# Writing the state products of a chunked scan to four column tiles of TensorE

## The chip, the cores and the metric

The kernel runs on one core of one Trainium2 chip. The metric is the device time of one launch in microseconds, lower is better. One further execution was profiled; all the rows below are read from its trace.

## The reference, cut to what matters

Eight images of 512 channels and 32 by 32 pixels go through four residual stages (L0 to L3), each `x = x + stage(groupnorm(x))`. L0, L2 and L3 are 1x1 convolutions (L0 with a local correlation beside it). L1 is a state space block: a 512 to 1536 projection, a short convolution along the tokens, a selective scan, gates, and a 512 to 512 projection. The scan is what the change touches:

```python
def step(h, inp):
    dA_t, dB_t, x_t, C_t = inp
    h = dA_t[:, :, None, :] * h + dB_t[:, :, None, :] * x_t[..., None]
    y_t = jnp.einsum('bhds,bhs->bhd', h, C_t)
    return (h, y_t)
```

There are 2 heads, 8 states per channel, 256 channels per head and N = 1024 tokens, in an order of each head's own.

## The kernel before, in words

Five engines run programs written out by hand, with semaphores between them (`wait` at L238). `image` is called for image 0, then in a loop for images 1 to 6, two at a time, then for image 7. The order of an engine's work is the order of its calls.

The scan of a head is done in 8 chunks of 128 tokens. A chunk adds to the state what its own tokens contribute: an 8 x 256 matrix, the **state product** of this chunk. It is one fp32 matmul with K = 128 tokens, 8 columns of weights (the slice `pfac[:, c * P + far : ... + S]`) and 256 moving columns (the channels). `FAR_GROUP` is (0, 0), so `far` is 0 for both heads. There are 7 per head (the last chunk's is not needed), 14 per image. The trace shows each fp32 matmul as two weight loads and two matmuls, so 28 records per image, 224 in all.

The order on TensorE in `image` around them, per head h:

- `scan_sums(h)`: sums of the time steps into banks 7 and 0. The last of its matmuls writes all of bank 0 and, for h = 1, waits until DVE has done six steps of head 0's state chain (semaphore `h_st`).
- pieces of the input projection (`piece(n)` is n steps of three fp16 matmuls with 512 columns each), with the transposes `factor_rows` (L1825) among them.
- `scan_inner(h)`: state products of chunks 0 to 3; eight 128 x 128 fp32 products of the factors into two banks; state products of chunks 4 to 6. Chunk 6 writes where chunk 0 was, and waits for `h_st` 2 of its head. `dh_mm` is raised after chunks 1, 3, 5 and 6.
- for head 0: `scan_sums(1)`, four steps of the projection, `scan_y(0)`. For head 1: a transpose of a bound (L1885), six steps, a one-row matmul that spreads the bound (it waits for DVE's L1075), then `scan_y(1)`, which gives the scan's output and waits for ACT's evacuations (L729).

`dh_bank` puts the products of chunks 0 and 1 into the two halves of a bank's free dimension, 2 and 3 into another's, 4 and 5 into bank 0, and 6 into the first bank again. All of them stand on PSUM partitions 0 to 7.

On DVE `scan_states(h)` is a chain over the chunks: a copy (L1544) and six dependent scalar_tensor_tensor steps (L1547), each `hst[c] = hst[c - 1] * gam[c] + product[c]` on 8 partitions and 256 elements, each waiting for the one before; then two additions (L1553) that make the matrix that `scan_y` needs. For head 0 the masks of head 1 (L1482 to L1486) stand ahead of that chain on DVE. Behind a head's chain, `scan_y(h)` reads `hst`. The output of head h goes through ACT (L729), a store to DRAM, and row gathers on POOL (L482), which bring the tokens back in image order for TensorE's transposes at L1902. POOL also builds a diagonal matrix (L471) in each head.

All matmuls other than transposes go through the helper at L1599.

Of the kernel before, what the change touches and what calls it, by code (L numbers as in the profile page):

```python
# [16 lines left out]
S, HEADS = 8, 2  # L17
DH = C // HEADS
# [63 lines left out]
def build(nc, d):  # L82
    at, packed = constants()
    with ExitStack() as ctx:
# [89 lines left out]
        ps = [ctx.enter_context(nc.psum_tensor(f"bank{i}", [P, HALF], F32)) for i in range(8)]  # L174
# [10 lines left out]
        dh_bank = lambda h, c: ((3, 4, 0, 3), (5, 6, 0, 5))[h][c // 2]  # L185
# [52 lines left out]
        def wait(eng, name, m, n):  # L238

            if n:  # L240
                eng.wait_ge(s[name], m * per[name] + n)
# [577 lines left out]
        def _(eng):  # L819
# [8 lines left out]
            c = 1  # L828
# [410 lines left out]
            def image(m, z, last=False):  # L1239
# [76 lines left out]
                if not (first or last):  # L1316
                    bias(m + 1, 0)
                scan_states(m, 0)
                scan_factors(m, 1, z)
                y_largest(m)  # L1320
                scan_states(m, 1)
                y_scale(m)

# [206 lines left out]
            def scan_states(m, h):  # L1530

                far = FAR_GROUP[h] * S
                hp = slice(far, far + S)
                if h == 0:
                    wait(eng, "h_zero", m, 1)
                else:
                    wait(eng, "y_mm", m, 4 * h)
                for c in range(NT - 1):
                    wait(eng, "dh_mm", m, 4 * h + c // 2 + 1)
                    inc = ps[dh_bank(h, c)][0:S, (c % 2) * DH:(c % 2 + 1) * DH]  # L1540
                    if c == 1:
                        wait(eng, "fac_gam", m, h + 1)
                    if c == 0:
                        eng.tensor_copy(hst[hp, 0, :], inc).then_inc(s["h_st"], 1)  # L1544
                    else:
                        wait(eng, "h_st", m, 7 * h + c)
                        STT(hst[hp, c, :], hst[hp, c - 1, :], gam[:, h, c:c + 1], inc, ALU.mult, ALU.add).then_inc(s["h_st"], 1)  # L1547

                wait(eng, "fac_diag", m, h + 1)
                for half in range(2):  # L1550
                    wait(eng, "mm_m", m, 2 * h + half + 1)
                    c = slice(half * HALF, (half + 1) * HALF)
                    TT(mmat[:, c], ps[m_bank[h] + half][:, :], diag[:, c], ALU.add).then_inc(s["m_ev"], 1)  # L1553
# [43 lines left out]
        def _(eng):  # L1597
            def mm(out, lhsT, rhs, start, stop, **kw):
                return eng.matmul(out, lhsT, rhs, start=start, stop=stop, skip_group_check=True, **kw)  # L1599
# [114 lines left out]
            def image(m, z, last=False):  # L1714
# [114 lines left out]
                def state_products(h, chunks):  # L1829

                    far = FAR_GROUP[h] * S
                    for c in chunks:
                        if c < 4 and c % 2 == 0:
                            wait(eng, "fac_ptq", m, 4 * h + 1 + c // 2)
                        if c == 4:
                            wait(eng, "fac_8", m, 5 * h + 1)
                        if c == 6:
                            wait(eng, "h_st", m, 7 * h + 2)
                        ins = mm(ps[dh_bank(h, c)][0:S, (c % 2) * DH:(c % 2 + 1) * DH],
                                 pfac[:, c * P + far:c * P + far + S], rows4[:, h, c, 0:DH], True, True)  # L1840
                        if c % 2 == 1 or c == NT - 2:
                            ins.then_inc(s["dh_mm"], 1)

                def scan_inner(h):

                    state_products(h, range(0, 4))
                    for half in range(2):
                        wait(eng, "fac_ptq", m, 4 * h + (3 if half == 0 else 4))
                        for c in range(4 * half, 4 * half + 4):
                            ins = mm(ps[m_bank[h] + half][:, (c % 4) * P:(c % 4 + 1) * P], pT[:, c * P:(c + 1) * P],  # L1850
                                     qT[:, c * P:(c + 1) * P], True, True)
                        ins.then_inc(s["mm_m"], 1)
                    state_products(h, range(4, NT - 1))
# [52 lines left out]
                def out_part(u, k):  # L1906
                    o, c = out_unit_of(u)
                    out, oc = ps[out_bank[u]][:, :], slice(o * P, (o + 1) * P)
                    if k >= 2:
                        return mm(out, w_out[:, k - 2, oc], gate[:, k, c], False, k == KC - 1)  # L1910
                    hi, lo = y_pair[:, k, u // KC, 0, :], y_pair[:, k, u // KC, 1, :]
                    mm(out, w_hi["out"][:, k, oc], hi, k == 0, False)
                    mm(out, w_hi["out"][:, k, oc], lo, False, False)
                    return mm(out, w_lo["out"][:, k, oc], hi, False, False)
# [37 lines left out]
                for u in range(5, 8):  # L1952
# [4 lines left out]
                    for k in range(KC):  # L1957
                        ins = out_part(u, k)
# [122 lines left out]
```

## Time and profile before

| | us |
|---|---|
| median of 3 runs | 1782.38 |
| the 3 runs | 1779.83 to 1783.09 |
| the profiled execution, its time | 1799.47 |
| its span (first to last instruction) | 1797.7 |
| TensorE busy in it | 1702.6 |
| DVE busy | 1148.6 |
| ACT busy | 892.4 |
| POOL busy | 412.0 |

The granted TensorE clock is 0.986 of full speed over the span. In rows of the timeline the first number is the start in us from the span's start, the second the length in us of what is merged in the row, then engine, line, operation, output and input names, shapes as stationary rows * columns and moving partitions x columns, and the count. In brackets stands the idle time of the engine before it and what ended it. A matmul's own length in a row contains the passage through the array, so that matmuls of a dense stream overlap: the distance from start to start is what one costs.

### The profile page before, as it was taken

Reading aid. Unit: us, or ns where it says so; the run is one execution under the profiler, and the core shown is the slowest. Engines: PE = TensorE matmul, PEld = TensorE weight load, DVE = VectorE, ACT = ScalarE, POOL = GpSimd, SP = SyncE. Lnnn points to the kernel's source line nnn. Section 1 sums busy time; section 2 is a strip of 40 time slices with the busy share of each in tenths; the row PEclk is TensorE's granted clock in tenths of the full one; section 3 lists DMA queues with packets and bytes.
Section 4 is the critical chain, followed back from the end, with each engine's and each line's share of the span. In section 5 each row is a group of like instructions: output and inputs, shape, how many; then the busy total and the mean of one; then the engine's idle time right before and its main releaser. Section 6 shows DMA issues by size and latency. Waiting matters only on the chain.

```text
span 1797.7 us, 24269 instructions
## 1 busy us (share of the span) xinstructions
PE 1702.6 (95%) x8725; PEld 944.7 (53%) x8725; DVE 1148.6 (64%) x2232; ACT 892.4 (50%) x1091; POOL 412.0 (23%) x423
## 2 busy tenths in 40 slices
PE   4689899999999999999999999999999999999988
PEld 3255554555545555456545565455554565555643
DVE  6879585656754666546865568555675467652675
ACT  4657354555255544455634644455535554545442
POOL 0303402134022321132220430213302232113220
PEclk9789999999999999999999999999999999999999
DMA  6203410233112331132301341023311233113201
GB/s 204 90 0 105 137 33 18 89 106 130 39 50 74 109 103 39 72 99 90 96 20 71 123 138 37 18 90 112 123 39 66 76 97 104 33 48 100 70 24 47
DMA packets 124077, 140.22 MB, mean 78 GB/s; under 512 B 52259, under 2 KB 101475, under 8 KB 123950
## 3 DMA queue, kind: packets, MB, share of 16 engines
q1 hardware_dynamic: 109902, 103.18, 18.0%
q0 software_dynamic: 12288, 34.68, 5.8%
q8 instruction: 75, 1.23, 0.3%
q10 hardware_dynamic: 1760, 0.71, 0.2%
q14 instruction: 52, 0.43, 0.1%
HBM read 78.52 MB, written 60.01 MB: 77 GB/s over the span
## 4 chain that ended last, share of the span: by engine, by line
PE 75%; DVE 9%; issue 5%; DMA 4%; ACT 3%; another core or an unknown queue 2%; POOL 2%; SPq 0%; DVEq 0%; POOLq 0%; ACTq 0%
PE bank L1599 71%; POOL rows L482 1%; PE bank L1767 1%; PE bank L1825 1%; DVE bn L915 1%; DMA rows<-d_y,rank 1%; DMA d_y<-buf_b 1%; PE bank L1902 1%; DVE res L1262 1%; DVE res L1260 1%; POOL d_scan L465 1%; DMA rows<-d_scan 1%; DMA x_even<-in_x 1%; ACT res L645 1%
## 5 line engine op out<-in xcount | busy, mean ns | idle before, releaser
L1599 PE MATMUL bank<-buf_a,win_hi 128*128 128x512 f16 x1536 | 461.5, 382 | 8.3 <-DVE buf_a L987 8.1
L1599 PE MATMUL bank<-buf_a,win_lo 128*128 128x512 f16 x768 | 293.2, 382 | 0.0
L1599 PE MATMUL bank<-buf_b,w_hi 128*128 128x512 f16 x960 | 288.3, 382 | 2.3 <-DVE buf_b L987 2.3
L1599 PEld LDWEIGHTS bank<-buf_a,win_hi 128*128 128x128 f16 x1536 | 150.7, 99 | 183.6 <-issue 13.6
L465 POOL DMA_INDIRECT d_scan<-rows,rank x128 | 125.5, 980 | 345.9 <-ACT rows L650 303.3
L1599 PE MATMUL bank<-buf_b,w_lo 128*128 128x512 f16 x480 | 183.0, 381 | 0.0
L1599 PE MATMUL bank<-buf_a,w_hi 128*128 128x512 f16 x576 | 171.3, 379 | 1.8 <-DVE x_odd L1230 1.7
L482 POOL DMA_INDIRECT rows<-d_y,rank x128 | 124.5, 973 | 136.9 <-DMA d_y<-buf_b 98.9
L1599 PEld LDWEIGHTS bank<-buf_b,w_hi 128*128 128x128 f16 x960 | 93.9, 99 | 112.3 <-DVE buf_b L987 3.0
L1599 PEld LDWEIGHTS bank<-buf_a,win_lo 128*128 128x128 f16 x768 | 75.7, 99 | 92.2 <-issue 2.8
L1599 PE MATMUL bank<-gate,w_out 128*128 128x512 f32 x256 | 120.3, 603 | 1.1 <-DVE gate L1339 1.1
L409 POOL TENSOR_TENSOR st<-st,minus_half 128x4 f32<-128x4 f32 x30 | 30.9, 1030 | 345.0 <-DVE st L973 249.5
L1599 PE MATMUL bank<-buf_a,w_lo 128*128 128x512 f16 x288 | 109.1, 379 | 0.0
L987 DVE TENSOR_TENSOR buf_a<-work,buf_a 128x1024 f16<-128x1024 f32 x68 | 83.0, 1221 | 29.7 <-ACT work L569 29.5
L987 DVE TENSOR_TENSOR buf_b<-work,buf_b 128x1024 f16<-128x1024 f32 x60 | 73.4, 1223 | 41.6 <-ACT work L569 33.5
L637 ACT ACTIVATE buf_b<-bank,par 128x512 f32<-128x512 f32 x64 | 49.7, 776 | 89.4 <-PE bank L1599 89.4
L637 ACT ACTIVATE res<-bank,par 128x512 f32<-128x512 f32 x64 | 48.8, 776 | 88.1 <-PE bank L1599 44.5
L1599 PEld LDWEIGHTS bank<-buf_a,w_hi 128*128 128x128 f16 x576 | 56.1, 99 | 64.4 <-DVE x_odd L1230 2.2
L625 ACT ACTIVATE work<-bank,par,y_bound 128x512 f32<-128x512 f32 x64 | 48.6, 773 | 79.7 <-PE bank L1599 77.3
L1599 PE MATMUL bank<-buf_a 128*128 128x256 f16 (+1 forms) x768 | 83.5, 270 | 2.8 <-DVE buf_a L987 2.1
L607 ACT ACTIVATE corr<-bank 96x512 f16<-96x512 f32 x16 | 9.5, 592 | 153.6 <-PE bank L1669 153.6
L1258 DVE TENSOR_SCALAR res<-buf_b,par 128x1024 f32<-128x1024 f32 x28 | 22.8, 813 | 91.7 <-ACT buf_b L637 91.7
(254 smaller groups left out, 3163.9 us busy)
## 6 DMA issues: line engine op xcount, KB each, us to landing
rows<-d_scan SPq DMA_DIRECT2D x16, 1092.0 KB, 5.7
d_y<-buf_b SPq DMA_DIRECT2D x64, 256.0 KB, 2.2
work<-in_x SPq DMA_DIRECT2D x24, 512.0 KB, 4.5
d_gram<-rows SPq DMA_DIRECT2D x32, 260.0 KB, 2.5
x_even<-in_x SPq DMA_DIRECT2D x16, 512.0 KB
x_odd<-in_x SPq DMA_DIRECT2D x16, 512.0 KB
out_x<-x_even SPq DMA_DIRECT2D x16, 512.0 KB, 2.6
out_x<-x_odd SPq DMA_DIRECT2D x16, 512.0 KB, 2.6
```

Of the source, the lines that this page charges most:

```text
L409: eng.tensor_tensor(st[g][:, :, 4], st[g][:, :, 3], minus_half.broadcast_to([P, KC]), ALU.pow).then_inc(s[f"gn_rstd{g}"], 1)
L465: eng.indirect_dma_start(d_scan[h], bass.IndirectOffsetOnAxis(ap=rank[:, h, t:t + 1], axis=0), rows4[:, h, t, :], None).then_inc(s[f"scatt ...
L482: eng.indirect_dma_start(ytok[h][:, t, :], None, d_y[h], bass.IndirectOffsetOnAxis(ap=rank[:, h, t:t + 1], axis=0)).then_inc(s[f"y_in{h}{2 ...
L625: act(tmp[:, u % 3, :], ps[out_bank[u]][:, :], ACT.Silu, bias=par[:, BOUT + o:BOUT + o + 1], scale=y_bound[:, 4:5]).then_inc(s["out_evac"], 1)
L637: act(dst, ps[in_bank[q]][:, :], ACT.Silu, bias=par[:, col:col + 1], scale=inv("in")).then_inc(s["in_evac"], 1)
L645: act(conv_out[:, k % 2, :], conv_out[:, k % 2, :], ACT.Silu).then_inc(s["conv_act"], 1)
L915: eng.bn_stats(bn[g][:, k, half, :], x[:, k, half * HALF:(half + 1) * HALF]).then_inc(s[f"gn_raw{g}"], 1)
L987: TT(lo[:, k, :], normed[:, k % 2, :], hi[:, k, :], ALU.subtract).then_inc(s[f"gn_split{g}"], 1)
L1258: TS(dst, src[:, 1:N + 1], w[1], par[:, BCONV + k:BCONV + k + 1], ALU.mult, ALU.add).then_inc(s["conv_mac"], 1)
L1260: STT(dst, src[:, 0:N], w[0], dst, ALU.mult, ALU.add).then_inc(s["conv_mac"], 1)
L1262: STT(dst, src[:, 2:N + 2], w[2], dst, ALU.mult, ALU.add).then_inc(s["conv_mac"], 1)
L1599: return eng.matmul(out, lhsT, rhs, start=start, stop=stop, skip_group_check=True, **kw)
```

## The change

The state product of chunk c is written to PSUM partitions 32 * (c % 4) to 32 * (c % 4) + 7 in place of 0 to 7, in the same bank and the same columns. The start partition of the output decides which 32 columns of the array the product uses, so chunks 0, 1, 2, 3 use column tiles 0, 1, 2, 3, and chunks 4, 5, 6 use tiles 0, 1, 2. DVE's chain reads the increments from there and keeps writing `hst` on partitions 0 to 7. No wait, no semaphore and no order changes.

```diff
--- before.py
+++ after.py
@@ -1537,7 +1537,7 @@
                     wait(eng, "y_mm", m, 4 * h)
                 for c in range(NT - 1):
                     wait(eng, "dh_mm", m, 4 * h + c // 2 + 1)
-                    inc = ps[dh_bank(h, c)][0:S, (c % 2) * DH:(c % 2 + 1) * DH]
+                    inc = ps[dh_bank(h, c)][32 * (c % 4):32 * (c % 4) + S, (c % 2) * DH:(c % 2 + 1) * DH]
                     if c == 1:
                         wait(eng, "fac_gam", m, h + 1)
                     if c == 0:
@@ -1836,7 +1836,7 @@
                             wait(eng, "fac_8", m, 5 * h + 1)
                         if c == 6:
                             wait(eng, "h_st", m, 7 * h + 2)
-                        ins = mm(ps[dh_bank(h, c)][0:S, (c % 2) * DH:(c % 2 + 1) * DH],
+                        ins = mm(ps[dh_bank(h, c)][32 * (c % 4):32 * (c % 4) + S, (c % 2) * DH:(c % 2 + 1) * DH],
                                  pfac[:, c * P + far:c * P + far + S], rows4[:, h, c, 0:DH], True, True)
                         if c % 2 == 1 or c == NT - 2:
                             ins.then_inc(s["dh_mm"], 1)
```

## Rows read from the trace of the kernel before

**Rows 1.** The page: span, TensorE's busy time, the chain that ended last by engine.
```profile
span 1797.7 us, 24269 instructions
PE 1702.6 (95%) x8725; PEld 944.7 (53%) x8725; DVE 1148.6 (64%) x2232; ACT 892.4 (50%) x1091; POOL 412.0 (23%) x423
...
PE 75%; DVE 9%; issue 5%; DMA 4%; ACT 3%; another core or an unknown queue 2%; POOL 2%; SPq 0%; DVEq 0%; POOLq 0%; ACTq 0%
```

**Rows 2.** Groups by line and form: matmuls and loads of the state products, even images.
```profile
L1599 PE MATMUL bank<-rows,x_even 128*8 128x256 f32 x112 | 27.4, 379 | 0.5 <-DVE work L1547 0.4
L1599 PEld LDWEIGHTS bank<-rows,x_even 128*8 128x8 f32 x112 | 8.5, 89 | 13.7 <-DVE work L1547 2.0 <-issue 1.3
```

**Rows 3.** Timeline of TensorE, image 2, head 1.
```profile
620.78 1.90 PE L1599 MATMUL bank<-rows,x_odd 128*8 128x256 f32 x8
622.60 2.05 PE L1599 MATMUL bank<-x_odd 128*128 128x128 f32 x16
624.58 1.46 PE L1599 MATMUL bank<-rows,x_odd 128*8 128x256 f32 x6
625.98 0.27 PE L1885 MATMUL bank<-cst,y_bound 128*1 128x128 f32 x1
...
630.06 0.38 PE L1599 MATMUL bank<-y_bound,cst 1*128 1x1 f32 x2
```

**Rows 4.** Timeline of TensorE's weight loads, image 2, head 1.
```profile
624.58 0.96 PEld L1599 LDWEIGHTS bank<-rows,x_odd 128*8 128x8 f32 x6
```

**Rows 5.** Timeline of DVE, image 2, head 1.
```profile
621.91 0.41 DVE L1544 COPY work<-bank 8x256 f32<-8x256 f32 x1 [1.16 <-PE bank L1599]
622.36 1.48 DVE L1547 SCALAR_TENSOR_TENSOR work<-work,gam,bank 8x256 f32<-8x256 f32 x3
625.74 1.48 DVE L1547 SCALAR_TENSOR_TENSOR work<-work,gam,bank 8x256 f32<-8x256 f32 x3 [1.90 <-issue]
...
628.88 0.14 DVE L1075 TENSOR_SCALAR y_bound<-y_bound 1x1 f32<-1x1 f32 x1
```

**Rows 6.** Timeline of TensorE, image 2, head 0.
```profile
605.60 0.60 PE L1599 MATMUL bank<-rows,x_odd 128*8 128x256 f32 x2 [0.18 <-DVE work L1547]
...
607.38 0.21 PE L1599 MATMUL bank<-rows,cst 128*8 128x8 f32 x2
607.61 1.13 PE L1599 MATMUL bank<-scan_tmp,cst 128*128 128x512 f32 x2
```

**Rows 7.** Timeline of DVE, image 2, head 0.
```profile
601.82 2.08 DVE L1483 TENSOR_TENSOR mv<-rows,cst 128x128 f32<-128x128 f32 x1
...
604.63 0.41 DVE L1544 COPY work<-bank 8x256 f32<-8x256 f32 x1
605.07 2.99 DVE L1547 SCALAR_TENSOR_TENSOR work<-work,gam,bank 8x256 f32<-8x256 f32 x6
```

**Rows 8.** Timeline of POOL, image 2: the diagonal of head 0, the second head's first gather.
```profile
601.79 1.96 POOL L471 TENSOR_TENSOR work<-md,cst 128x1024 f32<-128x1024 f32 x1 [8.14 <-DVE md L1528]
...
641.97 1.06 POOL L482 DMA_INDIRECT rows<-d_y,rank  x1 [10.43 <-DMA d_y<-buf_b]
```

**Rows 9.** Timeline of TensorE, head 0 of images 0, 1 and 7.
```profile
172.65 1.12 PE L1599 MATMUL bank<-scan_tmp,cst 128*128 128x512 f32 x2
...
395.49 1.13 PE L1599 MATMUL bank<-scan_tmp,cst 128*128 128x512 f32 x2
...
1675.33 1.10 PE L1599 MATMUL bank<-scan_tmp,cst 128*128 128x512 f32 x2 [0.40 <-DVE work L1547]
```

**Rows 10.** Timeline of DVE, head 0 of images 0 and 1.
```profile
169.66 3.33 DVE L1547 SCALAR_TENSOR_TENSOR work<-work,gam,bank 8x256 f32<-8x256 f32 x6
...
391.71 1.48 DVE L1547 SCALAR_TENSOR_TENSOR work<-work,gam,bank 8x256 f32<-8x256 f32 x3
393.86 1.48 DVE L1547 SCALAR_TENSOR_TENSOR work<-work,gam,bank 8x256 f32<-8x256 f32 x3 [0.67 <-PE bank L1599]
```

**Rows 11.** Timeline of TensorE, image 2, behind the second head's products.
```profile
634.49 0.67 PE L1599 MATMUL bank<-rows,work 128*128 128x256 f32 x2 [0.83 <-ACT buf_b L729]
...
648.91 1.09 PE L1902 MATMUL bank<-cst,rows 128*128 128x128 f32 x8 [0.74 <-DMA rows<-d_y,rank]
```

**Rows 12.** Timeline of ACT, image 2: the evacuation that the second head's output follows.
```profile
633.08 0.78 ACT L637 ACTIVATE res<-bank,par 128x512 f32<-128x512 f32 x1 [4.72 <-remote]
```

## The prediction

> **What bounds the kernel now.** I read the page first: TensorE is busy 1702.6 us of 1797.7, and the chain that ended last is 75% TensorE [rows 1]. So time taken off TensorE counts wherever TensorE waits for nobody behind it. Next the groups by form: the state products are 224 matmul records (112 in even images, as many in odd) of 379 ns and loads of 89 ns [rows 2]. Last the timeline around each head's products, for what TensorE meets when it comes earlier. Head 1 and head 0 differ there, and that difference is most of this forecast.
>
> **What a product costs.** Eight records fill 1.90 us; the last takes 0.379, so starts are (1.90 - 0.38) / 7 = 0.217 us apart; six fill 1.46, 0.216 apart [rows 3]. Call 0.217 a slot. A product is two slots, a head 7 products = 14 slots = 3.04 us, 16 heads 48.6 us. All run in the same 32 columns of the array, one after another.
>
> **What the change can remove.** Nothing is issued less: same matmuls, loads and semaphores. It can only let products on different column tiles run beside each other. The two passes of one product share a tile, so they stay a slot apart; issue is in order, so the next product's first pass can run beside the last pass of this one. n products then take n + 1 slots, not 2n: four take 5 of 8, three take 4 of 6. A head saves 5 slots = 1.085 us; all 16 would save 17.4. No row shows two tiles at work at once, so the bounds are 0 and 5 slots per head, below nothing in the rival further down. I take 5: loads of the products already run beside a matmul of the same tile (six loads end at 624.58 + 0.96 = 625.54, the last matmul starts 625.66 [rows 3, 4]), so loading needs no slot of its own, and another tile should not be harder.
>
> The Trainium skill ("TensorE: Matmul & The Clock Gate", Part 3) gives 2.38x for three column tiles of one-pass matmuls; no run here shows it. By its figure the groups of four and three would gain about as much or more than my slots, which are set by the two passes.
>
> **Head 1, 8 times.** Behind the products come a transpose, six steps of projection and the one-row matmul at 630.06, which waits for DVE's L1075, done at 629.02 [rows 3, 5]: 1.04 us of slack. TensorE comes 1.085 earlier, at 628.98. DVE comes earlier too: the second group starts 3 slots (0.65) sooner and its first pair takes 3 slots, not 4, so the step at 625.74 starts 0.87 sooner and L1075 ends at 628.15. The wait stays hidden. Chunk 6 waits for `h_st` 2, done at about 622.83 [rows 5], well before it is wanted. Then `scan_y(1)` waits 0.83 for ACT, and ACT itself was released at 633.08 by something the profile does not name [rows 11, 12]. I let it move with TensorE, for the evacuations, stores, gathers (from 641.97) and the transposes at 648.91 all hang on that output [rows 8, 11]. Head 1 saves 8 x 1.085 = 8.7 us. If the unnamed release stood still, the part of it behind ACT would be lost; that is rival (D).
>
> **Head 0, images 2 to 6.** Here DVE's chain starts late, at 604.63, behind the masks, one of which takes 2.08 us while POOL's 1.96 us multiplication runs [rows 7, 8]. TensorE already waits for it: chunk 6 at 605.60, then the last matmul of `scan_sums(1)` at 607.61, which needs six chain steps. Steps are (2.99 - 0.47) / 5 = 0.504 apart, so the fifth scalar_tensor_tensor ends at 605.07 + 4 x 0.504 + 0.47 = 607.56 [rows 6, 7]. Faster products only make TensorE wait earlier: nothing, in 5 images. In image 7 the same matmul waits 0.40 for DVE [rows 9]: nothing. In image 0 the fifth step ends at 169.66 + 4 x 0.572 + 0.47 = 172.42 and the matmul starts 172.65 [rows 9, 10]: 0.18. In image 1 DVE itself waits 0.67 for the products; without that gap its fifth step would end at 391.71 + 2.49 = 394.20, while the matmul starts at 395.49 [rows 9, 10]: the full 1.08.
>
> **DVE's side.** The chain reads PSUM partitions 32, 64, 96 and keeps its state on 0. The trace shows no such read. Each step already waits for the one before. Bounds: nothing, or the difference between the two spacings that the rows show for the same step, 0.572 - 0.504 = 0.07 [rows 7, 10]. Head 1 hides it (slack above 0.8); in head 0 of images 2 to 7 it would cost 5 x 0.07 x 6 = 2.1 us. I take nothing: the chain's spacing is the step's own 0.47 and 0.03 of hand-over, which leaves no room in which a partition offset shows.
>
> **Sum.** 8.7 + 1.1 + 0.2 = 10.0 us of the profiled 1799.5, giving 1789.5; of the median of 1782.4, which is 17.1 below the profiled time, 1772.4. Where those 17.1 lie no row tells. If part of them is in DVE's lateness in head 0, more of the 17.4 is to be had: low end 1765.0.
>
> **Rivals.** (B) The tiles do not run beside each other: a two-pass fp32 product may hold the whole array, or only the output address moves. For it: fp32 columns go at 0.217 us for 256, so the stream may be bound by something that the tiles share. Against it: nothing in the rows. Every distance stays 0.217: 1782.4.
>
> (C) Slower: a change of tile empties the array, as a change of tile shape does. The rows show that price: eight products end their slots at 620.78 + 8 x 0.217 = 622.52 and the next form starts at 622.60, 0.08 late [rows 3], about the 89 ns of a load [rows 2]. Head 1 has 3 + 2 changes: 5 x 0.089 x 8 = 3.6 us; images 0 and 1 add 0.9 in head 0; elsewhere DVE's lateness covers it. 1782.4 + 4.5 = 1786.9. It decides as soon as a load for another tile waits until the last matmul is through.
> The Trainium skill has a rule that would do this (same page, Part 3, "The mechanism"): a load runs beside a matmul in flight only when it goes to other rows of the array, and column tiles share their rows. By it the first pass of each next product would stand behind a bare load, and the sum would be (C)'s. The trace disagrees, for the loads above run beside a matmul on the same rows [rows 3, 4], so it gets a small chance.
>
> (D) The overlap is there, but half is eaten: by ACT's release standing still, or DVE's 2.1 us. About 5 us saved: 1777.4.
>
> **Numbers.** (A) is the forecast, slots as above: 0.50, 1772.4, own range 1765.0 to 1775.5. (D) 0.12. (B) 0.23. (C) 0.15. The range takes in the forecast's own, (D) and (B), with 2.6 us above (B) for the spread of the three runs (1779.8 to 1783.1): 1765.0 to 1785.0. It leaves out (C) and little else. What a measurement tells from no change is about 0.2%, 3.6 us. Faster 0.62, same 0.24, slower 0.14.
>
> **What would show each step.** In head 1 the eight product records fill about 5 x 0.217 + 0.16 = 1.25 us, not 1.90, and the six 1.03, not 1.46; the next form starts at +1.17 and not +1.82. In head 0 of images 2 to 6 the two matmuls that wait for L1547 stay at their distance from DVE's chain, with the idle before them grown from 0.18 to about 1. Steps of L1547 stay 0.50 apart. At 0.217 between all starts, (B) holds; at about 0.3 between products, (C). The forecast fails if the records shrink but the idle before L729's or L482's followers grows by as much; then (D).

## The result and the profile after

| | before | after |
|---|---|---|
| median of the runs | 1782.3 us (4 runs, 1779.8 to 1783.1) | 1771.0 us (4 runs, 1767.9 to 1771.1) |
| ratio, 95% interval | | 0.9934 [0.9919, 0.9949] |
| time of the profiled execution | 1799.5 us | 1771.1 us |
| its span | 1797.7 us | 1769.3 us |

The change makes the kernel 11.8 us faster by the ratio (1782.3 x 0.0066). It was forecast at 1772.4, range 1765.0 to 1785.0. The page of after, against [rows 1] (span, busy time of each engine, the chain that ended last):

```profile
span 1769.3 us, 24269 instructions
PE 1670.0 (94%) x8725; PEld 933.3 (53%) x8725; DVE 1151.0 (65%) x2232; ACT 894.0 (51%) x1091; POOL 411.9 (23%) x423
...
PE 75%; DVE 11%; issue 4%; DMA 4%; ACT 3%; POOL 2%; SPq 0%; DVEq 0%; POOLq 0%; ACTq 0%
```

The two spans shown are 28.4 us apart, and the medians only 11.3. The entry "another core or an unknown queue 2%" of [rows 1] is gone, and so is ACT's release by something unnamed [rows 12]. The kernel before was therefore profiled once more, as the first experiment (`again`): a span of 1783.0, with no such stall. The profile that the prediction was made on held about 15 us that belonged to that one execution. From here on, "before" in a comparison of places is `again`.

The state products in after, by form (columns: count | busy us, mean ns of one | idle before them, and what ended it), against the first of [rows 2]. The buffer `x_even` serves images 1, 3, 5 and 7, and `x_odd` images 0, 2, 4 and 6, as the timelines of image 2 show; the heading "even images" of [rows 2] has the name of the buffer for the number of the image:

```profile
L1599 PE MATMUL bank<-rows,x_odd 128*8 128x256 f32 x112 | 12.6, 385 | 10.1 <-DVE work L1547 10.1
L1599 PE MATMUL bank<-rows,x_even 128*8 128x256 f32 x112 | 12.2, 381 | 7.5 <-DVE work L1547 7.5
```

One record still takes 0.38 us, but the 112 fill 12.2 instead of 27.4: they lie on top of one another. The idle before them went from 0.5 (0.7 in `again`) to 7.5. Both halves of the story are here: the products overlap far more than was forecast, and in one of the two heads a wait has grown in their place.

Timeline of TensorE in after, image 2, head 1 (start, us, work; [idle before it <-releaser]), against [rows 3]:

```profile
617.47 0.62 PE L1599 MATMUL bank<-rows,x_odd 128*8 128x256 f32 x8
618.02 2.05 PE L1599 MATMUL bank<-x_odd 128*128 128x128 f32 x16
620.00 0.61 PE L1599 MATMUL bank<-rows,x_odd 128*8 128x256 f32 x6
620.55 0.27 PE L1885 MATMUL bank<-cst,y_bound 128*1 128x128 f32 x1
...
624.63 0.38 PE L1599 MATMUL bank<-y_bound,cst 1*128 1x1 f32 x2
```

Eight records in 0.62 us and the next form 0.55 after the first, where it had been 1.90 and 1.82 [rows 3]. Six in 0.61 and the next 0.55 later; `again` has 1.39 there. Four products on four tiles, or three on three, take the time of one: two slots and 0.12. From the first product to L1885 it is 3.08 us, and 5.20 in `again` (619.10 to 624.30): head 1 gains 2.12 us, 1.27 in its first group and 0.85 in its second.

Head 0 of the same image, TensorE and then DVE, against [rows 6, 7]:

```profile
597.26 0.62 PE L1599 MATMUL bank<-rows,x_odd 128*8 128x256 f32 x8
599.79 0.60 PE L1599 MATMUL bank<-rows,x_odd 128*8 128x256 f32 x4
602.27 0.60 PE L1599 MATMUL bank<-rows,x_odd 128*8 128x256 f32 x2 [1.88 <-DVE work L1547]
...
604.31 1.12 PE L1599 MATMUL bank<-scan_tmp,cst 128*128 128x512 f32 x2
```
```profile
601.30 0.41 DVE L1544 COPY work<-bank 8x256 f32<-8x256 f32 x1
601.75 3.02 DVE L1547 SCALAR_TENSOR_TENSOR work<-work,gam,bank 8x256 f32<-8x256 f32 x6
...
624.01 0.14 DVE L1075 TENSOR_SCALAR y_bound<-y_bound 1x1 f32<-1x1 f32 x1
```

The products are through just as early as in head 1, and then TensorE stands 1.88 us before chunk 6, where it stood 0.18. Chunk 6 reuses a bank that DVE's first step L1547 must have read; that step ends at 601.75 + 0.47 = 602.22, and the matmul starts at 602.27. From the first product to chunk 6 are 5.01 us (597.26 to 602.27), as before (`again`: 598.90 to 603.92). DVE sets this distance, so the whole gain of head 0 turned into waiting.

The last row of the fence above, L1075 at 624.01, ends at 624.15, 0.48 ahead of the one-row matmul at 624.63 that needs it: in head 1 the wait stayed hidden.

### The profile page after: what moved, and what is told of

It is laid out like the page before. It is cut to its first block, busy times and chain, and to the rows that moved or that the text cites. A ratio compares the mean times of both kernels' runs of the same rounds, so it can differ in the third digit from the quotient of the medians.

```text
span 1769.3 us, 24269 instructions
## 1 busy us (share of the span) xinstructions
PE 1670.0 (94%) x8725; PEld 933.3 (53%) x8725; DVE 1151.0 (65%) x2232; ACT 894.0 (51%) x1091; POOL 411.9 (23%) x423
## 4 chain that ended last, share of the span: by engine, by line
PE 75%; DVE 11%; issue 4%; DMA 4%; ACT 3%; POOL 2%; SPq 0%; DVEq 0%; POOLq 0%; ACTq 0%
PE bank L1599 72%; PE bank L1767 1%; POOL rows L482 1%; DMA rows<-d_y,rank 1%; DVE bn L915 1%; DMA d_y<-buf_b 1%; DVE gate L1138 1%; DMA rows<-d_scan 1%; PE bank L1902 1%; POOL d_scan L465 1%; PE bank L1825 1%; DVE res L1262 1%; DVE res L1260 1%; DVE work L1547 1%; DMA x_even<-in_x 1%
## 5 line engine op out<-in xcount | busy, mean ns | idle before, releaser
L1599 PEld LDWEIGHTS bank<-buf_a 128*128 128x128 f16 x768 | 73.3, 100 | 14.3 <-issue 6.4
```

## Experiments

Where a diff shows only a tile expression, both lines of the change (the product and DVE's read) have it. A median stands beside that of the kernel before in the same session.

### again: the kernel before, once more

No edit.

> The kernel before, once more, for a second profile of it. The shown profile took 17 us more than the median of its runs, and ACT and DVE sat in it for about 3 us per image before the second head's output with no releaser named (rows 12). If those stalls belong to that one execution, this profile has a span near 1781 us, no such stalls, and the eight-record group of head 1 still fills 1.90 us. If they belong to the kernel, they are here again and the change would have removed them.

Measured: 1783.8 against 1783.2, ratio 0.9999 [0.9988, 1.0011], profiled span 1783.0. TensorE and ACT of image 2:

```profile
603.92 0.60 PE L1599 MATMUL bank<-rows,x_odd 128*8 128x256 f32 x2 [0.18 <-DVE work L1547]
...
619.10 1.90 PE L1599 MATMUL bank<-rows,x_odd 128*8 128x256 f32 x8
...
628.49 0.78 ACT L637 ACTIVATE res<-bank,par 128x512 f32<-128x512 f32 x1 [1.81 <-PE bank L1599]
...
630.29 0.60 ACT L729 ACTIVATE buf_b<-bank 128x512 f32<-128x512 f32 x1 [1.02 <-PE bank L1599]
```

The products are as in [rows 3, 6]; in images 1 to 6 all chunks 6 of head 0 wait 0.17 to 0.18 us, and 2.62 in image 0, where the profile of before has no wait at all. ACT's L729 is released by TensorE, so it moves with TensorE; the release that did not, in [rows 12], was no part of the kernel's own order.

### h1_only and h0_only: the tiles in one head alone

```diff
-  32 * (c % 4)
+  32 * ((c % 4) * h)          # h1_only
+  32 * ((c % 4) * (1 - h))    # h0_only
```

> Only head 1 uses the four tiles, head 0 stays on partitions 0 to 7. Theory (products on four tiles run beside each other; TensorE saves 2.1 us in head 1 of each image; in head 0 it waits for DVE's chain either way, and the longer wait can cost clock): all of the gain or slightly more, 1765 to 1771 us. Rival (both heads give about half each): about 1776.5. Rival (the four tiles do nothing, the offset does): cannot be told from the theory here.

> Only head 0 uses the four tiles. Theory: TensorE reaches the wait for DVE's chain about 2 us earlier and gets nothing for it, 1781 to 1786 us, with the idle before chunk 6 near 1.9 us as after the change. Rival (both heads give about half each): about 1776.5.

Measured: `h1_only` 1766.0 against 1783.2, ratio 0.9894 [0.9877, 0.9911]. `h0_only` 1791.7, ratio 1.0043 [1.0028, 1.0059]. Head 1 alone saves 17.2 us, and 8 x 2.12 = 17.0 is what its timeline says. Head 0 alone costs 8.5, which none of the theories had. TensorE in `h0_only`, image 2 (timeline), and stretches of its span (us, PE busy (x), granted clock as a share of full speed, DMA share, GB/s):

```profile
607.28 0.60 PE L1599 MATMUL bank<-rows,x_odd 128*8 128x256 f32 x2 [1.88 <-DVE work L1547]
...
609.83 2.06 PE L1599 MATMUL bank<-scan_tmp,cst 128*128 128x512 f32 x2
```
```profile
609.50:614.00 4.50, 4.50 (x17) 0.75 0.00 0
...
1244.00:1250.00 6.00, 5.95 (x30) 1.00 0.01 3
```

The same 1.88 us of waiting as in after, and then a pair of matmuls takes 2.06 us instead of 1.12 and the granted clock is 0.75 over 4.5 us: for part of that stretch TensorE ran at the lower of its two levels (1.2 of 2.4 GHz). From head 0's first product to head 1's first product, image 2 takes 21.67 us here, against 20.20 in `again`. Images 1 to 4 all have 21.60 to 21.67; images 5 and 6 have 20.22, no more than before, and the stretch from 1244 us, in image 5, shows the clock at 1.00. Images 1 to 4 together lose 5.8 of the 8.5 us. Image 0 went from 22.97 to 24.66, but it can't be booked as the change's: with head 0 unchanged it took 19.76 us in the profile of before, 22.97 in `again` and 21.31 in `h1_only`.

In after the same thing happens in fewer images. Stretches behind chunk 6 of images 0, 1, 2 and 6, below them those of images 0, 1 and 6 in `again`, and last that of image 0 in `one_tile` (no overlap, see below):

```profile
174.00:181.00 7.00, 7.00 (x26) 0.67 0.00 0
...
394.00:399.00 5.00, 5.00 (x18) 0.70 0.02 3
...
602.00:607.00 5.00, 4.68 (x25) 1.00 0.00 0
...
1438.00:1444.00 6.00, 6.00 (x23) 0.72 0.00 0
```
```profile
174.00:181.00 7.00, 6.61 (x32) 1.00 0.00 0
394.00:399.00 5.00, 4.98 (x23) 1.00 0.00 0
...
1448.00:1454.00 6.00, 5.98 (x32) 1.00 0.00 0
```
```profile
174.00:181.00 7.00, 7.00 (x30) 0.76 0.00 0
```

A stretch of 5 us at 0.70 lacks 5 x 0.30 = 1.5 us of full speed, and images 1 and 6 are 1.46 longer than image 2 (21.67 against 20.21). Two images with the same wait, 1 and 2, differ in the clock that follows it, and no row says why. Of the 14 images 1 to 7 of `h0_only` and after, all with a wait of 1.85 to 1.89, six lose 1.4 to 1.5 us behind it and eight lose none; of the 14 of `two_alt` and `two_pairs` below, with waits of 1.00 to 1.47, none does. In image 0 the clock also falls in `one_tile`, behind a wait of 2.69, and in `again`, behind one of 2.62, it does not: what happens there is no evidence for the change.

### one_tile: all products on partitions 32 to 39

```diff
-  32 * (c % 4):32 * (c % 4) + S
+  32 * (1):32 * (1) + S
```

> All products on partitions 32 to 39: another tile than before, but one tile for all. Theory: nothing runs beside anything, eight records fill 1.90 us again, and DVE's chain steps stay at 0.50 us from start to start though they read another partition than they write: 1782 us, within 0.2%. Rival (leaving partition 0 is what helps): about 1771. Rival (the read across partitions costs DVE time that the change hides): 1783 to 1786.

Measured: 1784.7, ratio 1.0010 [0.9999, 1.0022]. TensorE of image 2, and the steps of DVE's chain (min/median/max ns):

```profile
605.61 0.60 PE L1599 MATMUL bank<-rows,x_odd 128*8 128x256 f32 x2 [0.29 <-DVE work L1547]
...
620.80 1.90 PE L1599 MATMUL bank<-rows,x_odd 128*8 128x256 f32 x8
...
L1547 DVE SCALAR_TENSOR_TENSOR work<-work,gam,bank x96: 471/472/474, 173.0 to 1682.4; 8x256 f32<-8x256 f32 x96
```

The tile's place gives nothing by itself: the gain needs several tiles. DVE's step takes 472 ns where `again` has 469, and chunk 6 waits 0.29, not 0.18. The image is 0.12 us longer in head 0 (20.32 against 20.20). The 1.5 us between the medians are less than a measurement can tell from nothing, yet the chunk-6 wait is DVE's and eight of them make 1 us.

The steps are not where that 0.12 comes from, for only one of them stands ahead of chunk 6. It is the start of the chain. DVE in image 2, `again` and then `one_tile`:

```profile
602.88 0.15 DVE L980 SCALAR_TENSOR_TENSOR st<-st 128x4 f32<-128x4 f32 x1
602.96 0.41 DVE L1544 COPY work<-bank 8x256 f32<-8x256 f32 x1
```
```profile
604.45 0.15 DVE L980 SCALAR_TENSOR_TENSOR st<-st 128x4 f32<-128x4 f32 x1
604.63 0.41 DVE L1544 COPY work<-bank 8x256 f32<-8x256 f32 x1
```

In `again` the copy starts 0.08 before the instruction ahead of it has ended; in `one_tile`, where it reads partition 32 and writes partition 0, it starts 0.03 behind that end. That is 0.10 us, the same in all 8 images. After copies chunk 0 from partition 0 and doesn't have it there, but it has it at the other end: its last step reads partition 64, and L1553 starts 0.03 behind it, where `again` has it 0.07 ahead of the last step's end (603.40 + 2.99 = 606.39):

```profile
603.40 2.99 DVE L1547 SCALAR_TENSOR_TENSOR work<-work,gam,bank 8x256 f32<-8x256 f32 x6
606.32 1.27 DVE L1553 TENSOR_TENSOR work<-bank,work 128x512 f32<-128x512 f32 x2
```
```profile
604.80 1.29 DVE L1553 TENSOR_TENSOR work<-bank,work 128x512 f32<-128x512 f32 x2
```

Every run with a last step that reads another partition has this in the heads concerned, and `two_alt`, whose last step reads partition 0, has it in none. In after the time that TensorE needs between the heads grows by only 0.01 to 0.03 from it (20.21 against 20.20 in image 2, where the clock stays up). The steps themselves take 467 to 482 ns in after, median 474; the bound of the prediction was 70 a step.

### two_alt and two_pairs: two tiles, in turn or in pairs

```diff
-  32 * (c % 4)
+  32 * (c % 2)          # two_alt: tiles 0 1 0 1
+  32 * (c // 2 % 2)     # two_pairs: tiles 0 0 1 1
```

> Two tiles in turn (partitions 0 and 32 by c % 2). Theory (a product holds its own tile for two slots of 0.217 us and products on different tiles start at once): four products take 4 slots, 0.97 us to the next form instead of 0.55 or 1.82; the group of three also 4 slots, 0.97. Head 1 saves 1.3 us per image, 10.4 in all: 1772 us, less up to 2 for slow clock in head 0. Rival (the number of tiles does not matter once there is a second one): 0.55 and 1766 to 1771.

> Two tiles in pairs (0, 0, 32, 32 for chunks 0 to 3; 0, 0, 32 for 4 to 6). If TensorE can start a product on a free tile past one that still waits for its own tile, four products take 4 slots, 0.97 us to the next form. If issue is strictly in order, the third starts only with the second, so four take 6 slots, 1.40 us, and the group of three 4 slots, 0.97. The device time then is about 1775 to 1777 in place of 1772.

Measured: 1775.6, ratio 0.9960 [0.9946, 0.9973], and 1776.4, ratio 0.9956 [0.9940, 0.9972], each against 1782.9. TensorE in head 1 of image 2, `two_alt` and then `two_pairs`:

```profile
614.96 1.04 PE L1599 MATMUL bank<-rows,x_odd 128*8 128x256 f32 x8
...
617.91 1.03 PE L1599 MATMUL bank<-rows,x_odd 128*8 128x256 f32 x6
618.87 0.27 PE L1885 MATMUL bank<-cst,y_bound 128*1 128x128 f32 x1
```
```profile
619.05 1.04 PE L1599 MATMUL bank<-rows,x_odd 128*8 128x256 f32 x8
...
622.01 1.03 PE L1599 MATMUL bank<-rows,x_odd 128*8 128x256 f32 x6
622.97 0.27 PE L1885 MATMUL bank<-cst,y_bound 128*1 128x128 f32 x1
```

Four products on two tiles take four slots and a little (0.97 to the next form) in either order. This is where the prediction's rule falls. If each matmul had to start after the one before it, tiles 0 0 1 1 could overlap only where product 2 meets product 3, and would need seven slots; if only products had to, six, as the expectation counts. They take four: the products on the second tile start beside those on the first, though a product on the first tile is ahead of them in the program and still waiting for its place. The single records of the trace show the same: the eight of `two_pairs` start in four pairs about 0.015 us apart (at 619.050 and 619.063, and last at 619.702 and 619.717), and that last pair are the two that raise `dh_mm`, the second passes of chunks 1 and 3. In these runs the time of a group is two slots times the most products on any one tile, and about 0.1.

The device times are a miss all the same. Rows and expectation agree on 10.3 us saved in head 1, but the medians fell by about 7 and 6.5, to where the expectation had `two_pairs` with strict order (1775 to 1777), which the rows rule out. In both profiles the clock stays up behind chunk 6 in images 1 to 7, so the missing 3 to 4 us are not explained.

### fill_wait: other work in the place of the wait

After, with the projection step that stood behind head 0's sums put ahead of the wait for chunk 6:

```diff
+                            if between:
+                                between()          # filler(1), for head 0
                             wait(eng, "h_st", m, 7 * h + 2)
...
                 scan_sums(1)
-                filler(1)
                 scan_y(0)
```

> The changed kernel with head 0's four steps of projection moved from behind scan_sums(1) to ahead of chunk 6, into the wait for DVE's chain. Theory (in head 0 the products' saving turns into a wait of 1.9 us, and the wait lowers TensorE's clock in some images at about 1.4 us each): the idle before chunk 6 goes from 1.88 us to near 0, scan_y(0) starts when DVE's L1553 is done, about 1.7 us earlier per image, no slow stretch after it: 1751 to 1757 us. Rival (the time between the chain's end and head 1 is set by another engine, so what TensorE does in the wait is free but gives nothing): 1764 to 1771.

Measured: 1764.3 against 1782.9, ratio 0.9894 [0.9875, 0.9912]; some 7 us faster than after. Chunk 6 no longer waits, and the distance between the heads' products in image 2 falls to 19.58 us. But the waits of TensorE (sum us, count, longest us) have a new one, and the time is the rival's, not the 1751 to 1757 of the theory:

```profile
PE bank L1599 <- ACT buf_b L729: 5.8, 8, 0.8
```

### two_banks and banks_fill: no bank is reused

Each group of tiles gets a bank of its own (four tiles of one bank stand in the same columns), so chunk 6 needs no wait for DVE, nor does chunk 4 for bank 0. The wait for `h_st` ahead of the last matmul of `scan_sums(1)` goes too:

```diff
-        dh_bank = lambda h, c: ((3, 4, 0, 3), (5, 6, 0, 5))[h][c // 2]
+        dh_bank = lambda h, c: ((3, 4), (5, 6))[h][c // 4]
...
-  (c % 2) * DH:(c % 2 + 1) * DH
+  0:DH
...
-                        wait(eng, "h_st", m, 6)
...
-                        if c < 4 and c % 2 == 0:
-                            wait(eng, "fac_ptq", m, 4 * h + 1 + c // 2)
-                        if c == 4:
-                            wait(eng, "fac_8", m, 5 * h + 1)
-                        if c == 6:
-                            wait(eng, "h_st", m, 7 * h + 2)
+                        if c % 4 == 0:
+                            wait(eng, "fac_ptq", m, 4 * h + 1 + c // 4)
```

`banks_fill` puts `filler(1)` ahead of `scan_sums(1)` as well.

> The changed kernel with chunks 0 to 3 of a head in one bank and 4 to 6 in a second one, each on its own partitions and all in columns 0 to 255. Nothing is reused, so chunk 6 has no step of the chain to wait for, and bank 0 is free for scan_sums(1), which no longer waits for six steps. Theory: TensorE waits only ahead of scan_y(0), for L1553, under 1 us per image: 1751 to 1757 us, as with the filled wait. Rival (another engine sets head 1): 1764 to 1771. Rival (the four writes to one bank disturb each other): the eight-record group takes longer than 0.55 us from its start to the next form.

> The two-bank form with the four steps ahead of scan_sums(1), which waited 0.96 us and up to 2.9 us for DVE's masks of head 1 (L1486). Theory: that wait is filled, no slow clock in image 0 to 7 behind it; what is left is the wait for ACT's L729 behind DVE's L1500, about 1 us per image: 1757 to 1762. Rival (DVE and ACT set the start of head 1's work anyway): the same 1762 to 1764 as the two-bank form.

Measured: `two_banks` 1762.5 against 1782.9, ratio 0.9885 [0.9870, 0.9900]. `banks_fill` 1760.4 against 1784.0, ratio 0.9878 [0.9860, 0.9896]. These are the lowest medians, but the intervals overlap, with each other's and with those of `fill_wait` and `h1_only`. `two_banks` lies between its theory and its rival, nearer to the rival's time, in which another engine takes the wait over; `banks_fill` lies within its theory's. The four writes to one bank don't disturb each other: the eight records take 0.55 us to the next form here too (596.05 to 596.60). In both the distance between the heads' products in image 2 is 19.5 us, 0.7 less than before; not the 2.12 that the products gave. What takes the rest, in `two_banks`, TensorE and then ACT in image 2:

```profile
600.16 0.49 PE L1599 MATMUL bank<-mv,cst 128*128 128x128 f32 x2 [0.96 <-DVE scan_tmp L1486]
...
608.86 0.67 PE L1599 MATMUL bank<-rows,work 128*128 128x256 f32 x2 [0.57 <-ACT buf_b L729]
```
```profile
606.04 2.19 ACT L715 ACTIVATE x_odd<-x_odd 128x1024 f32<-128x1024 f32 x2 [5.18 <-DVE x_odd L1500]
608.14 0.58 ACT L729 ACTIVATE buf_b<-bank 128x512 f32<-128x512 f32 x1
```

TensorE first waits for the masks of head 1 (L1486), which stand ahead of the chain on DVE, and then for ACT's L729, which stands behind L715, which stands behind DVE's L1500. One wait of DVE's schedule was taken away and two others of it came out. In `banks_fill` the wait for L1486 is filled as expected, but one for DVE's L1553 stands in its place, 8.5 us over the 8 images, which was not expected; images 1 to 7 are as long between the heads as in `two_banks`, 19.5 to 19.8, so the filler gave them nothing.

### h0_fill and before_fill: is it the filler or the clock?

`h0_only` and the kernel before, each with the filler moved as in `fill_wait`.

> Tiles in head 0 alone, which took 1791.7 us, with the four steps of projection moved ahead of chunk 6. Theory (what made head 0 alone 8.5 us slower is the lower clock that follows TensorE's wait of 1.9 us for DVE's chain; with work in the wait it doesn't fall): 1779 to 1783 us, no stretch behind chunk 6 with a granted clock below 1.00 in images 1 to 7. Rival (the tiles or the reads across partitions cost time by themselves in head 0): stays above 1787.

> The kernel before with that move alone, no other tile. Theory: TensorE waits only 0.2 us there, so the move has nothing to fill: 1780 to 1784. Rival (the move by itself is worth the 7 us that the filled wait gained on the change): about 1776.

Measured: `h0_fill` 1779.1 against 1784.0, ratio 0.9973 [0.9962, 0.9984]; `before_fill` 1791.8, ratio 1.0045 [1.0030, 1.0059]. The filler takes 12.6 us off `h0_only`. The images show two parts. In images 5 to 7, where the clock of `h0_only` had stayed up, the distance between the heads falls by 0.6 to 0.7 (20.22 to 19.59): that is the filler's own, some 5 us over 8 images, and all that `h0_fill` gains on the kernel before. In images 1 to 4 it falls by 2.0 to 2.1 (21.67 to 19.59 in image 2), 1.4 more. In the profile of `h0_fill` the clock stays up behind chunk 6 in images 0 to 7. That bears out the clock as the cost of head 0. The other was a miss: the same move makes the kernel before 7.8 us slower, where nothing or a small gain was expected. In it, TensorE and then DVE of image 2:

```profile
606.09 0.60 PE L1599 MATMUL bank<-rows,x_odd 128*8 128x256 f32 x2
...
613.25 0.67 PE L1599 MATMUL bank<-rows,work 128*128 128x256 f32 x2 [1.09 <-ACT buf_b L729]
```
```profile
606.82 0.47 DVE L1547 SCALAR_TENSOR_TENSOR work<-work,gam,bank 8x256 f32<-8x256 f32 x1 [1.21 <-PE bank L1599]
...
609.18 2.36 DVE L1500 TENSOR_TENSOR x_odd<-bank,amat 128x1024 f32<-128x1024 f32 x2 [0.70 <-PE bank L1599]
```

The filler ahead of chunk 6 makes chunk 6 late (7.46 us behind head 0's first product, against 5.02 in `again`), DVE's last step waits 1.21 us for it, so L1500 starts 1.9 later (10.55 behind that product, against 8.61), then L715, then L729, and TensorE waits for that 1.09 us, 8.7 us over the 8 images. Without the tiles there was no wait to fill. So `fill_wait` is no gain of its own that the change happened to meet: each needs the other.

## Why the prediction was right, and which of its steps were not

The total came out 1.4 us from the forecast by errors that cancel: head 1 gave 8.3 us more than its term, head 0 took 3 us or more where 1.3 were credited, and the rest was not traced. That the number was met is luck; that products on different tiles run beside each other, and that head 0's part in images 2 to 6 turns into waiting, was not.

**Slots.** "n products then take n + 1 slots" failed: four on four tiles take two slots and 0.12 us, three take the same. It rested on "issue is in order, so the next product's first pass can run beside the last pass of this one". `two_pairs` shows that a product on a free tile does not wait for the start of those ahead of it. The term for head 1, 8 x 1.085 = 8.7 us, measured 17.0 (8 x 2.12) and 17.2 (`h1_only`).

**Head 0.** Nothing saved in images 2 to 6 was right (20.20 us in image 2 before, 20.21 after), for the reason given, DVE's lateness; only the wait grew to 1.88, not to about 1, as the products gained twice as much. Image 6 even lost 1.47, like image 1. The credits of 0.18 and 1.08 us for images 0 and 1 failed. ([rows 9, 10] give 172.65 - 172.42 = 0.23 for image 0, not 0.18.) They were read in the one profile in which chunk 6 waits for nothing in these two images; in `again` image 1 waits 0.18 for DVE like the others, and in after it loses 1.47. What the forecast lacked altogether is that a longer wait lowers the granted clock behind it. In after, against `again`, that is 1.47 us in images 1 and 6 each, 2.9 together. Image 0 is 1.79 longer, 0.11 of it ahead of chunk 6, but it varies by more than that without the change. Head 1's 17.0 less 2.9 and 1.8 is 12.3; measured are 11.3 by the medians, 11.8 by the ratio and 13.7 by the two profiled spans. The rest of the 13.7 is in places that the change doesn't touch: after reaches head 0 of image 0 1.3 us later than `again`, and is 3.0 faster than 8 x 2.12 on the ways from head 1 to the next image's head 0, or to the end. Those ways differ by up to 1.8 us each between `again` and `one_tile` as well, although the products take the same time in both. Head 0 alone (`h0_only`) costs 8.5, in after less, for there fewer images meet the low clock; how many do is not settled by anything that these profiles show.

**Head 1's cover.** Right: the slack ahead of the one-row matmul went from 1.04 to 0.48, and ACT moved with TensorE. The 0.83 us wait of TensorE for L729 [rows 11] was no part of the question: `again` has none of these waits either.

**DVE's side.** Taken as nothing, since the 0.03 of hand-over "leaves no room". The steps do stay within 0.01 of theirs, but the price is at the ends of the chain: 0.10 us where the step or copy there reads another partition than it writes, for the overlap with DVE's neighbouring instruction is lost (`one_tile`). In after that is once a head, and nearly all of it is hidden.

**The rivals.** (B) and (C) fall with the eight records in 0.62 us. (C)'s price of 0.09 a change of tile would put 0.27 into a group with three changes; after shows at most 0.12 there (0.55 less two slots), of which 0.08 stood there before, with no change of tile [rows 3], and `two_alt` with three changes takes no longer than `two_pairs` with one (1.04 both). The Trainium skill ("TensorE: Matmul & The Clock Gate", Part 3, "The mechanism") has loads run beside a matmul only when it goes to other rows. The trace disagrees: the loads and the matmuls of all eight share their rows, and the loads' records of the group in head 1, image 2, fill 0.12 us beside the matmuls' 0.62:

```profile
617.47 0.12 PEld L1599 LDWEIGHTS bank<-rows,x_odd 128*8 128x8 f32 x8 [0.17 <-issue]
```

The Trainium skill's figure of 2.38x for three tiles ("TensorE: Matmul & The Clock Gate", Part 3, "Measured speedup vs the span model"; the row is for 32 columns and 512 moving, and says nothing of passes) was taken to give "about as much or more" than the slots. Here four products go from 1.82 to 0.55 us, 3.3x, and three from 1.39 to 0.55, 2.5x. By that figure of the Trainium skill an estimate for three products is 6 / 2.38 = 2.5 slots. The prediction's rule gave 4, and the trace has 0.55 / 0.217 = 2.5. (D) foresaw that half is lost, to ACT or to DVE's steps; of the 17 us that head 1 gives alone 5 to 7 were lost. The profiles put 2.9 of them down to the clock behind DVE's wait; the others are in image 0 or not traced.

## What to carry to other kernels

Small products that use few columns of the array are worth spreading over its column tiles: in these runs the time of a group was that of the products on its fullest tile, in either order that was tried. Before doing so, find for each place who releases TensorE next. Where it is a slower engine's chain, the time saved becomes a wait, and the wait can cost more than it replaces, as the granted clock falls behind it; so change only the places with slack (`h1_only` beats the whole change by 5 to 7 us), or take the wait away with it (`banks_fill` beats it by about 10). And profile the kernel before twice: terms of 1 us read from a single execution can be that execution's own, and so can image 0's, which changed by 3 us from one profile of the same kernel to the other.

## What the runs showed of the hardware

- Four fp32 products of two passes each on four column tiles take 0.55 us to the next form's start, one tile 1.82. Two tiles take 0.96 for three products (617.91 to 618.87), alternating or not.
- A product on a free tile starts past one that still waits for its own tile (`two_pairs`: 0.97 us for four products on tiles 0 0 1 1, where strict order would need six or seven slots, 1.3 or 1.5).
- A wait of 1.88 us of TensorE, with work packed on both sides, was followed by a fall of the granted clock in six images of `h0_only` and after (0.70 to 0.75 over 4.5 to 6 us in the three shown) and by 1.00 in eight; the six are 1.4 to 1.5 us longer. Waits of 1.00 to 1.47 at the same place were followed by 1.00 in all of 14 images.
- DVE reads PSUM at partition 32 into a step whose other operand is on partition 0 in 472 ns, at 0 in 469 (`one_tile`, `again`). An instruction of DVE that reads PSUM at partition 32 or 64 and writes at 0 doesn't overlap with an independent neighbour: 0.03 us between them, where the same pair at partition 0 overlaps by 0.07 to 0.08.
